# A four-stage layer kernel: dispatch list inverted in four quarters, V products moved into units 12 to 15, mixer out-projection in three float32r passes

## The reference

```
x = L0_attn_hidden_states                       # (2, 1024, 256)
xn = _layernorm(x)
s = mixer(xn, W_in, conv_w, conv_b, dt_bias, A_log, D, norm_weight, W_out)
#   ... Y = Y_diag + Y_off + D * x ; g = y * silu(gate)
#   gg = g / rms(g per group) ; out = einsum('bli,di->bld', gg * norm_weight, W_out)
g = _silu(hadamard_ffn(xn, ...))
x = x + s * g
xn = _layernorm(x)
s = causal_attention(xn, Wq, bq, Wk, bk, Wv, bv, Wo, bo)       # V = xn @ Wv.T + bv
g = _silu(moe(xn, gate_w, expert_gate_up, expert_down, shared_gate_up, shared_down, ...))
#   top 4 of 16 experts per token, weights normalized ; shared expert * sigmoid
x = x + s * g
```

## Time and profile before

| | us |
|---|---|
| median of 3 runs | 2422.06 (2418.85 to 2424.81) |
| the profiled execution | 2423.18, its span 2421.4 |
| PE busy | 2188.3 (90%) |
| DVE busy | 1834.8 (76%) |
| POOL busy | 1228.3 (51%) |
| ACT busy | 1153.8 (48%) |
| mean granted clock of PE | 0.958 |

### The profile page before, as it was taken

How to read it: one execution, slowest core, us unless ns; L and a number is a source line. 1 busy time by engine, 2 the same in 40 slices (tenths; PEclk the granted TensorE clock), 3 DMA queues, 4 the chain that set the end, 5 groups by cost and what they waited for, 6 DMA issues and landing times. The chain is left out here.

```text
span 2421.4 us, 38962 instructions
## 1 busy us (share of the span) xinstructions
PE 2188.3 (90%) x12970; PEld 1687.8 (70%) x12970; DVE 1834.8 (76%) x3270; ACT 1153.8 (48%) x2419; POOL 1228.3 (51%) x1323
## 2 busy tenths in 40 slices
PE   4995899999999999999999999988977998899972
PEld 3784688888888888888888888867766776344432
DVE  4885788888888888888888888855663444888745
ACT  1332455555555555555555555533342333466660
POOL 3543366566565664665665655544333333999000
PEclk9998699999999999999999999998988999899996
DMA  2002000000000000000000000025115555333214
GB/s 94 1 14 76 32 3 3 33 3 2 33 3 33 3 3 33 3 3 33 3 3 34 3 3 3 3 106 191 46 53 132 177 177 145 107 121 119 76 62 159
DMA packets 76886, 128.89 MB, mean 53 GB/s; under 512 B 22331, under 2 KB 54683, under 8 KB 74683
## 3 DMA queue, kind: packets, MB, share of 16 engines
q1 hardware_dynamic: 69827, 107.65, 13.1%
q0 software_dynamic: 6864, 18.75, 3.2%
HBM read 91.82 MB, written 46.92 MB: 57 GB/s over the span
## 5 line engine op out<-in xcount | busy, mean ns | idle before, releaser
L957 DVE SCALAR_TENSOR_TENSOR mix_cv<-mix_pp,mix_cw,mix_cv 128x384 f32<-128x384 f32 (+4 forms) x864 | 492.7, 570 | 25.4 <-ACT mix_cv L880 4.5
L804 PEld LDWEIGHTS mix_pyd<-mix_xdt,mix_lm 128*128 128x128 f32 x2048 | 248.1, 192 | 56.6 <-issue 53.1
L880 ACT ACTIVATE mix_cv<-mix_pp,mix_cb,mix_cw 128x384 f32<-128x384 f32 (+1 forms) x288 | 182.4, 633 | 204.9 <-PE mix_pp L80 204.9
L78 PE MATMUL mix_pp<-l0in_XH,mix_wx_lo 128*128 128x384 f32 (+2 forms) x576 | 239.1, 415 | 40.5 <-DVE mix_ss L946 25.4
L743 POOL TENSOR_TENSOR mix_xdt<-mix_xtok,l_dt 128x512 f32<-128x512 f32 x128 | 133.8, 1045 | 277.3 <-ACT mix_xtok L907 277.3
L736 POOL TENSOR_TENSOR mix_t<-mix_t,mix_xd 128x512 f32<-128x512 f32 x112 | 144.5, 1290 | 218.8 <-DVE mix_t L971 153.3
L855 PE MATMUL mix_pgt<-mix_wo,mix_gt 128*128 128x256 f32 x1024 | 244.9, 382 | 2.9 <-issue 2.2
L804 PE MATMUL mix_pyd<-mix_xdt,mix_lm 128*128 128x64 f32 x2048 | 243.4, 272 | 2.5 <-DVE mix_lm L1007 2.5
L1915 DVE TENSOR_REDUCE att_tops<-att_psc 128x1 f32<-128x512 f32 (+3 forms) x384 | 189.6, 549 | 46.7 <-PE att_psc L1863 32.2
L886 ACT ACTIVATE mix_pp<-mix_cv 128x384 f32<-128x384 f32 (+1 forms) x288 | 133.0, 462 | 161.8 <-DVE mix_cv L957 159.1
L855 PEld LDWEIGHTS mix_pgt<-mix_wo,mix_gt 128*128 128x128 f32 x1024 | 184.1, 190 | 31.2 <-issue 9.2
(11 more groups left out here) (388 smaller groups left out, 5808.7 us busy)
## 6 DMA issues: line engine op xcount, KB each, us to landing
mix_w_raw<-in_w_in SPq DMA_DIRECT2D x8, 1280.0 KB
y_d<-exp_ys SPq DMA_DIRECT2D x79, 128.0 KB, 1.7
a_part<-att_sums SPq DMA_DIRECT2D x32, 256.0 KB, 5.1
mix_ll<-cs SPq DMA_DIRECT2D x384, 4.0 KB
q<-q SPq DMA_DIRECT2D x12, 512.0 KB, 4.5
k<-k SPq DMA_DIRECT2D x12, 512.0 KB, 4.8
att_qs<-q SPq DMA_DIRECT2D x32, 192.0 KB
att_ks<-k SPq DMA_DIRECT2D x32, 192.0 KB
```

Of the source, the lines that this page charges most:

```text
L78: pe.matmul(out, l_lo, r_hi, start=start, stop=False)
L804: last = pe.matmul(pyd[:, h * HP:(h + 1) * HP], lm[p % 2][:, h, :], xdt[p % 2][:, h * HP:(h + 1) * HP], start=True, stop=True)
L880: act.activation(conv_tile(k), pp[k % 2][:, halo:cols], ACT.Identity, bias=cb[:, it // 2, ct:ct + 1], scale=cw[:, it // 2, ct, 3:4]).then_ ...
L957: last = dve.scalar_tensor_tensor(out, of, cw[:, g, ct, 3 - d:4 - d], out, ALU.mult, ALU.add)
```

## The change

**Mixer.** The out-projection is `matmul3`: `gt` is kept as `g_hi` (ACT writes it from the transposed y, then `gt` as before) and `g_lo` (POOL, `gt - g_hi`), `wo` as `wo_hi` and `wo_lo` (three `split` pieces in place of one, now in slots 4 to 14). `xd`, `t1` and `gt` have one buffer in place of two.

**Middle.** The inversion is done in quarters of 16 columns, before the gate-ups of units 20 to 23; `opos`, `same` and `val` have one buffer of a quarter's size each. V is made in units 12 to 15, two lots of two tiles per unit, in the bank `pr`. h shares its space with the experts' row buffers. POOL issues the first four gathers at the end of the middle block; wd is loaded behind them, in two pieces of columns; the load of wg moves behind the last store of xn.

```diff
-                            last = pe.matmul(pgt[:, 0:D], gt[e % 2][:, k * P:(k + 1) * P], wo[:, e // 16 % 2, k, :],
-                                             start=k == 0, stop=k == NX - 1)
+                            last = matmul3(pe, pgt[:, 0:D], g_hi[:, k * P:(k + 1) * P], g_lo[:, k * P:(k + 1) * P],
+                                           wo_hi[:, e // 16 % 2, k, :], wo_lo[:, e // 16 % 2, k, :], k == 0, k == NX - 1)
...
-                        act.activation(gt[e % 2][:, :], pxt[:, :], ACT.Copy).then_inc(gts_done, 1)
+                        wait(act, g_split, e)
+                        wait(act, op_done, e)
+                        act.activation(g_hi[:, :], pxt[:, :], ACT.Copy)
+                        act.activation(gt[:, :], pxt[:, :], ACT.Copy).then_inc(gts_done, 1)
...
-                    if 0 <= c < NC and 4 <= c % 16 < 13 and c // 16 < G0 - 1:
+                    if 0 <= c - 2 < NC:
+                        e = c - 2
+                        pool.wait_ge(gts_done, e + 1)
+                        wait(pool, op_done, e)
+                        pool.tensor_tensor(g_lo[:, :], gt[:, :], g_hi[:, :].bitcast(F32), ALU.subtract).then_inc(g_split, 1)
+                    if 0 <= c < NC and 4 <= c % 16 < 15 and c // 16 < G0 - 1:
...
-                        wait(pool, y_done, c - 1)
-                        pool.tensor_tensor(by_head(xd[o]), by_head(xtok[o]),
+                        wait(pool, y_done, c)
+                        pool.tensor_tensor(by_head(xd), by_head(xtok[o]),
...
-        DONE_AT = (0,) * 10 + (3, 9, 15, 21, 27, 32, 39, 42, 48, 50, 52, 54, 55, 57, 58, 61)
-        PREFIX_AT, IDX_AT = 16, (23, 25)
+        DONE_AT = (0,) * 10 + (3, 9, 15, 21, 27, 32, 39, 43, 49, 51, 54, 57, 60, 63, 65, 65)
+        PREFIX_AT, IDX_AT, V_AT = 16, (20, 21, 22, 23), 12
...
+                def values(v):
...
+                    wait(pe, vs, v)
+                    for t in (2 * v, 2 * v + 1):
+                        rows = slice(t * P, (t + 1) * P)
+                        for k in range(KD):
+                            last = matmul3(pe, pr[:, t % 2 * D:(t % 2 + 1) * D], XH[:, k, rows], XL[:, k, rows], wqh[:, k, 2 * D:],
+                                           wql[:, k, 2 * D:], k == 0, k == KD - 1)
+                    last.then_inc(mv, 1)
...
+                        pe.wait_ge(vs, NT // 2)
...
                         project(n - QK_AT)
+                    if 0 <= n - V_AT < NB:
+                        values(2 * (n - V_AT))
...
+                    if 0 <= n - V_AT < NB:
+                        values(2 * (n - V_AT) + 1)
...
+                    elif j < 60 and j % 3 == 0:
+                        i = (j - 48) // 3 * NH2
+                        wait(dve, idx_done, (j - 48) // 3)
...
+                pool.wait_ge(dv, 65)
+                pool.wait_ge(rows_out, 16 * NB)
+                for j, sem in enumerate(xs_in):
+                    pool.indirect_dma_start(xs[:, j, :], None, xn_rows,
+                                            bass.IndirectOffsetOnAxis(ap=idx[:, j:j + 1], axis=0)).then_inc(sem, 16)
...
+                sp.wait_ge(dv, 65)
+                for sem in xs_in:
+                    sp.wait_ge(sem, 16)
+                sp.dma_start(W[0:EI // 2, B:B + 4352], wd_d[:, 0:4352]).then_inc(w2_ld, 16)
...
-                sp.wait_ge(idx_done, 2)
-                sp.wait_ge(dv, 61)
-                sp.dma_start(W[0:EI // 2, WG_COLS:], wd_d).then_inc(w2_ld, 16)
+                sp.dma_start(W[0:EI // 2, B + 4352:], wd_d[:, 4352:]).then_inc(w2_ld, 16)
```

More of the change, by code:

```diff
@@ L584, in mixer @@
         cv = s.sb("cv", [P, NCT, T // 2])
-        xtok, xdt, xdtd, xd, t1, y, gt = (
-            [s.sb(f"{n}{j}", [P, GX]) for j in range(2)] for n in ("xtok", "xdt", "xdtd", "xd", "t1", "y", "gt"))
+        xtok, xdt, xdtd, y = ([s.sb(f"{n}{j}", [P, GX]) for j in range(2)] for n in ("xtok", "xdt", "xdtd", "y"))
+        xd, t1, gt = (s.sb(n, [P, GX]) for n in ("xd", "t1", "gt"))
         btok = [s.sb(f"btok{j}", [P, N0]) for j in range(2)]
@@ L726, in split @@
                         pool.tensor_tensor(lo, raw, hi.bitcast(F32), ALU.subtract).then_inc(done, 1)
-                for piece in range(9):
+                for piece in range(11):
                     split(0, piece)
@@ L1042, in middle @@
         dh, dl = (s.sb(n, [P, NS, D], F32R) for n in ("dh", "dl"))
[L1043 removed]
+        h = [xs[:, 2 * a:2 * a + 2, :].rearrange("p a d -> p (a d)") for a in range(2)]
         hh, hl = ([s.sb(f"{n}{a}", [P, TB], F32R) for a in range(NH)] for n in ("hh", "hl"))
@@ L1071, in middle @@
         tilef, posf = keyb[:, 0, :], keyb[:, 1, :]
[L1072 to L1075, removed]
+        NQ = 4
+        NH2 = NPAIR // NQ
+        opos = at(0, 1024).bitcast(BF16).rearrange("p (j q) -> p j q", j=NH2)
+        same = at(1024, 640).bitcast(BF16).rearrange("p (j q) -> p j q", j=NH2)
+        val = at(1664, 1280).bitcast(BF16).rearrange("p (j v q) -> p j v q", j=NH2, v=2)
+        before = W[0:1, B + 2944:B + 2944 + SLOTS1 * E].rearrange("p (j e) -> p j e", e=E)
         wq = at(4608, 1536).rearrange("p (k n) -> p k n", k=KD)
@@ L1380, in _ @@
                             act.activation(F[:, t, :], F[:, t, :], ACT.Copy, scale=sig[:, t:t + 1])
-                    if n in (22, 24):
-                        half = n // 2 - 11
-                        act.wait_ge(dv, (54, 57)[half])
-                        wait(act, idx_done, half)
-                        for t in range(NT // 2):
+                    if n + 1 in IDX_AT:
+                        q = IDX_AT.index(n + 1)
+                        act.wait_ge(dv, 50 + 3 * q)
+                        wait(act, idx_done, q)
+                        for t in range(NT // NQ):
                             last = act.activation(val[:, 4 * t:4 * t + 4, 0, :], same[:, 4 * t:4 * t + 4, :], ACT.Copy,
-                                                  scale=float(half * NT // 2 + t))
+                                                  scale=float(q * NT // NQ + t))
                         last.then_inc(val_done, 1)
@@ L1606, in experts @@
         s = Scope(nc, ctx, "exp")
-        xs, ys = ([s.sb(f"{n}{a}", [P, D]) for a in range(NX_RING)] for n in ("xs", "ys"))
+        xs = [xrows[:, a, :] for a in range(NX_RING)]
+        ys = [s.sb(f"ys{a}", [P, D]) for a in range(NX_RING)]
         xt = [s.sb(f"xt{a}", [P, KD, P]) for a in range(2)]
@@ L1627, in _ @@
             def _(pool):
-                for j in range(NJ):
+                for j in range(NX_RING, NJ):
                     wait(pool, xt_done, j - NX_RING + 1)
@@ L2113, in build @@
         stored = [s.sem(f"stored{a}") for a in range(NR3)]
+        xs, xs_in = s.sb("xs", [P, 4, D]), [s.sem(f"xs_in{a}") for a in range(4)]
         VN = s.sb("VN", [P, 2 * H1 * (NT // 2) * (DH + 1)])
```

130 lines of the change are left out of this document (65 added, 65 removed).

## The result

The changed kernel takes 2438.49 us (median of four runs; three of them lie between 2437.28 and 2439.6, with a median of 2437.38) against 2421.49 for the kernel before in the same runs. The fourth, a disturbed execution of 5497.91 us, stands in that median but is left out of the comparison, which gives a ratio of 1.0063, 95% interval 1.0049 to 1.0077. It is slower by 15 to 17 us, 12 to 19 by the interval; the forecast was 11 (2433 us). The profiled execution has a span of 2437.8 us against 2421.4, +16.4.

The account below looks back on a forecast made before the run. PE and DVE, with its POOL round trip, were taken to bound the mixer nearly equally, and a chain through the engines the middle. Mixer -19 and middle +30 (+16 +2.5 +16 -4.5) made +11: 2433 us, own range 2426 to 2442.

Parts of the forecast that it names:

- The bound in the mixer: Mixer slots: PE and DVE with its POOL round trip end within 1.4 us over eight slots; faster PE soon meets DVE.
- The mixer's -19: Mixer out-projection: PE saves 38 us, 20 passed on as DVE's wait for the exponential goes; +1.3 at the last chunk.
- The cover of the new POOL and ACT work: Mixer: POOL's new subtraction, 10.3 us per eight slots, is hidden in its 18.0 us of idle time waiting for ACT.
- V products, +16: Units 12 to 15: V products add 4.05 us to each of four units, +16 in all; bounds 7 and 17.
- The frame: Units 12 to 15: PE's V lots, DVE's evictions, then list and subtraction follow in series, 10.7 us in place of 6.65.
- the list: Units 12 to 15: DVE's dispatch-list work, 3.40 us per unit, comes after the V evictions and covers nothing.
- Quarters, +2.5 and +16: Middle inversion: unit 19 comes 2.5 later; units 19 to 23 gain +16 from rings of 14.5 us, the first 14.
- Gathers and wd, -4.5: Experts' start: first down projection 40 us after h(23), not 46.7, -7; PE's restart at the lower clock +2.5.
- Sum: Whole kernel: middle +30 (bounds +15 and +37) with the mixer's -19 gives +11, 2433 us.
- Rival 1: Mixer: PE is the bound after all and all 38 us are passed on, 2415 or 2400 us; chance 0.24.
- rival 2: Units 20 to 23: PE keeps full clock, ring 11.9, middle +21 or +15, 2418 to 2424 us; chance 0.23.
- rival 3: Mixer: POOL becomes late with subtraction and splits, the mixer gains nothing, 2453 us; chance 0.12.

Follow-up runs that it names:

- experiment 7: Changed kernel with only the high-by-high pass of the out-projection's three, the two low-part products left out: 2481.99 us in a single run.
- experiment 8: Changed kernel without ACT's second copy, POOL subtracting the high part from itself so g's low part is zero: 2435.36 us in a single run.
- experiment 2: Changed kernel with V made after the loop as before, in two banks by turns: 2422.67 us, ratio 1.0001 to the kernel before.
- experiment 3: Changed kernel with 20 identity matmuls on PE ahead of each quarter's inversion: 2430.1 us, ratio 1.0027 to the kernel before.
- experiment 10: Changed kernel with POOL's subtraction for h's low part in units 19 to 22 held until DVE's comparisons and scaling are done: 2435.86 us, ratio 1.0053.
- experiment 1: Kernel before with only the mixer's part of the change, middle and experts as before: 2409.46 us, ratio 0.9945.
- experiment 4: Kernel before with the new mixer and the four gathers at the middle block's end, wd not waiting for them: 2407.87 us, ratio 0.9941.
- experiment 5: Changed kernel with each of wd's two pieces loaded as 80 rows and 8 rows in place of 88: 2433.65 us, ratio 1.0049.

## Why the prediction was right, step by step

- **The bound in the mixer.** Right, and sharper than argued: in the changed kernel PE sets none of seven of the eight slots (experiment 7), and four of the eight were not PE's before it either (the table).
- **The mixer's -19.** Right sign, mis-sized: the slots gave 12.1 (1314.40 to 1302.30), 0.78 per eight slots in place of 1.3. The step that failed is "with PE earlier, DVE's wait for the exponential goes". It went from 1.4 to 1.1; what more was gained lies in instructions that follow closer on one another. In the changed kernel's slots it stands in three of eight, 0.33 to 0.37 each, behind a chain ACT (L935), PE's decays (L803, which waits 1.4 us for L935 in eight slots), ACT (L940), DVE. It did not go with less of PE's work (1.6 in experiment 7, of which 0.9 fall in the slot at the lower clock) or of ACT's (1.0 in experiment 8). That the chain's own length sets it is what I read from these rows; no run shortened the chain. The cover of the new POOL and ACT work held: in the eight slots nothing waits for `g_lo` (PE does for 4.7 us in the whole run, 2.5 of them at the last chunk), and without ACT's copy nothing is faster.
- **V products, +16.** +14: 39.65 against 25.6 from h(12) to h(16). The frame was right (10.0 per unit in three of the four, against 10.7; the fourth went from 5.67 to 9.65). The term that is 0.7 too large is the list: one of its pieces, L1460, took 1.20 us in the earlier trace rows's unit, where POOL was at work beside it (read from the rows, not tested), and 0.42 now that the list comes later. Experiment 2 undoes the term.
- **Quarters, +2.5 and +16.** +18.2, in other shares: h(19) comes 0.8 later in place of 2.5, and from h(19) to h(23) it is 56.95 in place of 39.6, +17.3. Ring for ring 13.3, 14.3, 14.0, 15.4 against 14 and 14.5. PE's idle time of 5 us in each ring (5.6 measured, 4.3 in the first), and the lower level of the clock behind it, were as said; gate-up took 3.3 to 4.7 us, 4.0 in the mean, where 4.4 was reckoned; experiment 3 shows the clock to be 8 us of it. Two terms were off against each other: `opos` took 2.29, not 2.79, and `same` 2.43, not 1.5, since POOL was at work (experiment 10). That the total came so near (18.2 against 18.5) is in part luck.
- **Gathers and wd, -4.5.** The first down projection comes 40.8 us after h(23) in place of 46.7 plus the 1.3 of h: -7, as forecast. From it to the attention's first matmul it is 205.1 against 202.3, +2.8, where the restart at the lower level was forecast at 2.5; the first down projection alone takes 2.07 in place of 1.03. wd took 22.3 us where 22 were reckoned.
- **Sum.** Middle and experts +28 in place of +30, mixer -12 in place of -19: +16 in place of +11. The runs divide it alike: the mixer -13 (experiment 1), the quarters and the end with gathers and wd +13 (from experiment 1 to 2), the V products +15 to 16 (experiment 2). Rival 1 (PE bounds the mixer) fell in the mixer's rows and experiment 7, rival 2 (full clock in the quarters) in the trace: 0.79, rival 3 (POOL late) in the mixer's rows.

## What to carry to other kernels

A saving on an engine that is busy 98% of the time can be worth a third of its size (12 of 38 us here): add up what the next engine does with its round trips included, and expect that to be the floor. Moving work from a tail into a loop is only a gain if the loop has a hole there; here the tail lay under a load, and the loop had a chain through every engine. When one buffer serves a sequence of pieces, each piece costs the whole ring, and the idle time in it can lower PE's clock, which was 8 of the 17 us here.

## What the runs showed of the hardware that was not expected

- Less work for PE made the kernel slower: with 0.95 us less per slot the mean granted clock fell from 1.00 to 0.84 and 0.72 in two successive slots, and a slot of 8.4 us took up to 12.5 (experiment 7, a single run).
- A comparison on DVE (bf16, 128x1280) takes 1.49 us alone and 2.43 when POOL's subtraction is running as it starts; delaying POOL gives 1.49 in all four (experiment 10). The Trainium skill, "SBUF — State Buffer", section "SBUF: two separate sides", says that the two engines share a pair of ports as a lock for a whole instruction, and that the one that comes second stands still. The rows agree: the subtraction ran from 1786.20 to 1787.96, `same` began at 1786.89 and ended at 1789.32, 1.36 after it, near its 1.49 alone.
- Four gathers issued from 0.9 us before to 3.1 us after a large load of another queue landed 10.6 to 21.6 us after issue, and 2.7 to 3.1 in the changed kernel, where the load waits for them (experiment 4).
- POOL's queue stood at the end of the block until its gathers had landed, 25.1 us in experiment 4, and the other engines passed that end only then, at 1831.7.
- A load of 88 rows kept 64.3% of the engines busy, and the same load as 80 and 8 rows 96.1%, with 2.47 MB moved in 12 us in place of 1.81 (experiment 5).
